# Softmax attention in a two-layer kernel: reciprocals taken over DRAM and applied by GpSimd, the causal mask added by VectorE

## The reference, cut to what matters

```python
latent_kv = x @ w_kv_down
kv = latent_kv @ w_kv_up
k, v = (kv[..., :HD], kv[..., HD:])
q = (x @ w_q).reshape(Bx, Tx, N_HEAD, HEAD_SIZE)
scale = HEAD_SIZE ** (-0.5)
att = jnp.einsum('bqhd,bkhd->bhqk', q, k) * scale
causal = jnp.tril(jnp.ones((Tx, Tx), dtype=bool))
att = jnp.where(causal, att, -jnp.inf)
att = jax.nn.softmax(att, axis=-1)
y = jnp.einsum('bhqk,bkhd->bqhd', att, v)
y = y.reshape(Bx, Tx, HD)
return y @ w_out
```

## Time and profile before

| | us |
|---|---|
| median of 3 runs (1919.01 to 1919.22) | 1919.13 |
| the profiled execution | 1919.19 |
| its span, first to last instruction | 1917.1 |
| TensorE busy | 1703.5 (89%) |
| VectorE busy | 1362.2 (71%) |
| ScalarE busy | 1000.8 (52%) |
| GpSimd busy | 619.1 (32%) |
| softmax attention, its first product to its last division | 1196.1 to 1740.5 |

### The profile page before, as it was taken

The page is one execution under the profiler, slowest core; times in us unless marked ns, Lnnn a source line. Parts: engine busy times, 40 slices in busy tenths (PEclk is TensorE's granted clock), DMA queues, the critical chain, the costliest instruction groups (busy, mean ns, idle before and its releaser), DMA issues. The chain is left out here.

```text
span 1917.1 us, 42317 instructions
## 1 busy us (share of the span) xinstructions
PE 1703.5 (89%) x15702; PEld 1445.2 (75%) x15702; DVE 1362.2 (71%) x3230; ACT 1000.8 (52%) x2618; POOL 619.1 (32%) x975
## 2 busy tenths in 40 slices
PE   4599999899999999999988598999999999998895
PEld 3477778787877778877876365688888888888794
DVE  4688777877788777877775475566666666664777
ACT  2355555555555555565543354556566656652353
POOL 6455345543555335543451122000000000001653
PEclk9799999999999999999988799999999999999898
DMA  6212331323222332323320200990000000003232
GB/s 216 59 51 65 75 86 49 68 59 85 65 56 65 75 87 46 74 67 75 83 50 23 90 1 5 183 14 2 2 2 2 1 2 1 2 2 107 65 93 76
DMA packets 150338, 106.78 MB, mean 56 GB/s; under 512 B 34132, under 2 KB 138648, under 8 KB 149240
## 3 DMA queue, kind: packets, MB, share of 16 engines
q1 hardware_dynamic: 147640, 98.95, 23.7%
q0 software_dynamic: 2496, 5.13, 0.8%
HBM read 86.06 MB, written 17.99 MB: 54 GB/s over the span
## 5 line engine op out<-in xcount | busy, mean ns | idle before, releaser
L593 POOL TENSOR_TENSOR kfull<-kt,pair_rows 128x512 f32<-128x512 f32 x128 | 143.6, 1122 | 517.2 <-ACT kt L381 513.5
L361 PE MATMUL ps<-xT,taps 128*128 128x128 f32 x2048 | 276.8, 278 | 0.1
L853 ACT COPY wt<-ps 32x128 f32<-32x128 f32 x512 | 131.7, 257 | 263.9 <-PE ps L748 256.9
L361 PEld LDWEIGHTS ps<-xT,taps 128*128 128x128 f32 x2048 | 258.7, 196 | 7.6 <-issue 7.2
L1687 DVE TENSOR_REDUCE b_nmax<-ps 128x1 f32<-128x128 f32 (+7 forms) x256 | 180.6, 752 | 72.9 <-PE ps L1524 72.9
L896 DVE TENSOR_TENSOR prod<-ps,mt 128x128 f32<-128x128 f32 x512 | 147.4, 288 | 78.6 <-PE ps L759 62.7
L748 PE MATMUL ps<-ident,w 128*128 128x128 f32 x512 | 162.9, 318 | 34.6 <-ACT wt L853 18.5
L1664 POOL COPY b_spread<-b_inv 128x256 f32<-128x256 f32 x64 | 25.8, 402 | 513.2 <-DVE b_inv L1690 513.2
L899 DVE TENSOR_REDUCE w<-prod 128x32 f32<-128x128 f32 x512 | 146.5, 286 | 17.5
L748 PEld LDWEIGHTS ps<-ident,w 128*128 128x128 f32 x512 | 88.1, 172 | 84.9 <-DVE w L899 73.6
L1616 ACT ACTIVATE b_prob_long<-ps,b_nmax 128x1024 f32<-128x1024 f32 (+3 forms) x128 | 121.4, 953 | 55.7 <-DVE b_nmax L1687 55.7
(11 more groups left out here) (308 smaller groups left out, 3843.2 us busy)
## 6 DMA issues: line engine op xcount, KB each, us to landing
decay<-ends_dram SPq DMA_DIRECT2D x256, 128.0 KB, 5.5
gn<-near_dram SPq DMA_DIRECT2D x32, 384.0 KB, 6.9
slots_dram<-zero SPq DMA_DIRECT2D x1, 9216.0 KB, 59.3
rr<-rates_dram SPq DMA_DIRECT2D x32, 256.0 KB, 4.5
sq<-rstd_dram SPq DMA_DIRECT2D x16, 512.0 KB, 3.6
wtap<-in_taps SPq DMA_DIRECT2D x4, 1024.0 KB, 11.2
f_w<-in_f_w SPq DMA_DIRECT2D x2, 2048.0 KB, 10.4
s_xb<-slots_dram SPq DMA_DIRECT2D x46, 64.5 KB, 1.8
```

The lines of the kernel that those rows point to most:

```text
L361: mm = pe.matmul(part, lhsT=taps[:, tap, t * P:(t + 1) * P], rhs=xT[:, :, columns(at_next) - LOOK + tap:columns(at_next) - LOOK + tap + TS ...
L593: nc.gpsimd.tensor_tensor(kfull[:, n % 4, :, :], kt[:, n % 2, :].unsqueeze(1).to_broadcast([P, G, P]), cst["pair_rows"][:, :].unsqueeze(2) ...
L853: nc.scalar.copy(wt[rows, b, :], ps[rows, 2, 0:P]).then_inc(wt_kept[b], 1)
```

## The change

Four things, in one diff:

1. The reciprocals no longer pass through GpSimd's copy, TensorE's transpose and ScalarE's copy. SyncE stores the 128x4 reciprocals to DRAM (`recips_dram`, two slots) and, when they have landed, loads them back with two broadcasts over 64 partitions each, into `recipT` in the layout of the values.
2. ScalarE copies the values out of bank 7 into `yT` (`keep_values`), and GpSimd multiplies `yT` by `recipT` in place. TensorE's values of the next unit wait for ScalarE's copy (`o_kept`). VectorE's `divide` is gone.
3. TensorE's mask products are gone. VectorE adds the mask to the diagonal tile in the bank and waits for that addition (`masked`) before it takes the row's maximum. The waits for copied banks now stand in `scores`, at the first product into each bank.
4. SyncE's two fill transfers are issued by ScalarE instead, after its first eight projection copies and ahead of its first exponential.

Besides, VectorE's reciprocal waits until the store of the unit two before has landed, and the 16-bit identity is no longer built in the first stage.

```diff
@@ softmax_attention
-        spread = sb("spread", [P, 2, 4, AD])
-        recipT = sb("recipT", [P, 2 * P])
+        recipT = sb("recipT", [P, 2, 2 * P])
+        recips_dram = nc.dram_tensor("recips_dram", (2, 4, P), F32).ap()
...
+        def y_of(w):
+            hp, b, k = units[w]
+            return y_row[:, hp, b, k:TT - k:TT - 1 - 2 * k, :, :]
@@ tensor
-                def masks(w):
-                    for long in (False, True):
-                        for h in range(2):
-                            n = tiles(w, long)
-                            if w:
-                                for c, (of_long, lo, hi, bank) in enumerate(chunks(w - 1)):
-                                    if bank == (2 * h + 1 if long else 4 + h):
-                                        wait_kept_chunk(w - 1, c)
-                            pe.matmul(scores_of(w, long, h)[:, (n - 1) * P:n * P], lhsT=cst["ident16"][:, :],
-                                      rhs=cst["above_diag"][:, :], start=True, stop=False, skip_group_check=True)
...
-                                if w and not diagonal and c0 == 0:
+                                if w and c0 % 512 == 0:
                                     for c, (of_long, lo, hi, bank) in enumerate(chunks(w - 1)):
-                                        if bank == 2 * h:
+                                        if bank == (2 * h + c0 // 512 if long else 4 + h):
                                             wait_kept_chunk(w - 1, c)
...
-                                               rhs=kT[rows, f, b * T + c0:b * T + c1], start=not diagonal, stop=True,
+                                               rhs=kT[rows, f, b * T + c0:b * T + c1], start=True, stop=True,
...
                     if w:
-                        pe.wait_ge(y_done, w)
+                        pe.wait_ge(o_kept, w)
...
-                def turn_recips(w):
-                    pe.wait_ge(spread_done, w + 1)
-                    for long in range(2):
-                        mm = pe.transpose(ps[:, 7, (2 + long) * P:(3 + long) * P],
-                                          spread[:, w % 2, 2 * long:2 * long + 2, :].rearrange("p h c -> p (h c)"),
-                                          cst["ident"][:, :])
                     mm.then_inc(o_done, 1)
@@ scalar
-                def keep_recips(w):
+                def keep_values(w):
                     act.wait_ge(o_done, w + 1)
-                    nc.scalar.copy(recipT[:, :], ps[:, 7, 2 * P:4 * P]).then_inc(recip_kept, 1)
+                    nc.scalar.copy(y_of(w), ps[:, 7, 0:2 * P].rearrange("p (i n t) -> p i n t", i=2,
+                                                                        n=P // TS)).then_inc(o_kept, 1)
...
+                slots = blank[2].rearrange("(k p) e -> p k e", p=P)
+                act.wait_ge(fill_made, 2)
+                nc.scalar.dma_start(slots[:, :, 0:C], blank[1][:, :].unsqueeze(1).to_broadcast(
+                    [P, slots.shape[1], C])).then_inc(filled, 16)
+                nc.scalar.dma_start(slots[:, :, C:ROW], blank[0][:, :].bitcast(F32).unsqueeze(2),
+                                    allow_slow_non_contiguous=True).then_inc(filled, 16)
                 for w in range(W):
                     for j in range(4):
                         exponent(w, j)
@@ sync
-                sp.dma_start(slots[:, :, 0:C], ...)  and  sp.dma_start(slots[:, :, C:ROW], ...)
+                for w in range(W):
+                    slot = recips_dram[w % 2]
+                    if w >= 2:
+                        sp.wait_ge(y_done, w - 1)
+                    sp.wait_ge(recip_done, w + 1)
+                    sp.dma_start(slot.rearrange("j q -> q j"), inv[:, w % 2, :],
+                                 allow_slow_non_contiguous=True).then_inc(recip_stored, 16)
+                    sp.wait_ge(recip_stored, 16 * (w + 1))
+                    for h in range(2):
+                        sp.dma_start(recipT[AD * h:AD * h + AD, w % 2, :].rearrange("c (l q) -> c l q", l=2),
+                                     slot[h:4:2, :].partition_broadcast(AD)).then_inc(recip_in[w % 2], 16)
@@ gpsimd
-                    pool.wait_ge(recip_done, w + 1)
-                    nc.gpsimd.tensor_copy(spread[:, w % 2, :, :], inv[:, w % 2, :].unsqueeze(2).to_broadcast(
-                        [P, 4, AD])).then_inc(spread_done, 1)
+                    pool.wait_ge(recip_in[w % 2], 32 * (w // 2 + 1))
+                    pool.wait_ge(o_kept, w + 1)
+                    nc.gpsimd.tensor_tensor(y_of(w), y_of(w), recipT[:, w % 2, :].rearrange(
+                        "p (i n t) -> p i n t", i=2, n=P // TS), ALU.mult).then_inc(y_done, 1)
@@ vector
                         dve.wait_ge(s_done, 4 * w + j + 1)
+                        n = tiles(w, j // 2)
+                        diagonal = scores_of(w, j // 2, j % 2)[:, (n - 1) * P:n * P]
+                        nc.vector.tensor_tensor(diagonal, diagonal, cst["above_diag"][:, :], ALU.add).then_inc(masked, 1)
+                        dve.wait_ge(masked, 4 * w + j + 1)
                         nc.vector.tensor_reduce(nmax[:, w % 2, j:j + 1], scores_of(w, j // 2, j % 2), axis=AX.X, op=ALU.max,
                                                 negate=True).then_inc(max_done, 1)
                     dve.wait_ge(exp_done, 4 * w + 4)
+                    if w >= 2:
+                        dve.wait_ge(recip_stored, 16 * (w - 1))
                     nc.vector.reciprocal(inv[:, w % 2, :], total[:, w % 2, :]).then_inc(recip_done, 1)
-                    if w:
-                        divide(w - 1)
```

More of the change, by code:

```diff
@@ L1555, in values @@
                                 cols = slice(AD * h, AD * h + AD)
-                                pe.matmul(ps[cols, 7, long * P:(long + 1) * P], lhsT=v[:, f, b * TT + j, cols],
-                                          rhs=probT[:, at_probT(w, long, h * n + j), :], start=(j == 0), stop=(j == n - 1),
-                                          skip_group_check=True)
-                def turn_recips(w):
-                    pe.wait_ge(spread_done, w + 1)
-                    for long in range(2):
-                        mm = pe.transpose(ps[:, 7, (2 + long) * P:(3 + long) * P],
-                                          spread[:, w % 2, 2 * long:2 * long + 2, :].rearrange("p h c -> p (h c)"),
-                                          cst["ident"][:, :])
+                                mm = pe.matmul(ps[cols, 7, long * P:(long + 1) * P], lhsT=v[:, f, b * TT + j, cols],
+                                          rhs=probT[:, at_probT(w, long, h * n + j), :], start=(j == 0),
+                                               stop=(j == n - 1), skip_group_check=True)
                     mm.then_inc(o_done, 1)
@@ L1585, in _ @@
                 pe.wait_ge(piece_kept_v, 4)
-                masks(0)
                 for w in range(W):
@@ L1597, in _ @@
                         next_piece(w, n)
-                    if w + 1 < W:
-                        masks(w + 1)
                 values(W - 1)
-                turn_recips(W - 1)
             @block.scalar
@@ L1633, in _ @@
                     if w:
-                        keep_recips(w - 1)
+                        keep_values(w - 1)
                     hp = w // PW
@@ L1644, in _ @@
                                 "p (j t) -> p j t", t=P)).then_inc(t_kept_a, 1)
-                keep_recips(W - 1)
+                keep_values(W - 1)
             @block.sync
             def _(sp):
-                slots = blank[2].rearrange("(k p) e -> p k e", p=P)
-                sp.wait_ge(fill_made, 2)
-                sp.dma_start(slots[:, :, 0:C], blank[1][:, :].unsqueeze(1).to_broadcast(
-                    [P, slots.shape[1], C])).then_inc(filled, 16)
-                sp.dma_start(slots[:, :, C:ROW], blank[0][:, :].bitcast(F32).unsqueeze(2),
-                             allow_slow_non_contiguous=True).then_inc(filled, 16)
+                for w in range(W):
[9 more added lines that the diff above has]
+                                     slot[h:4:2, :].partition_broadcast(AD)).then_inc(recip_in[w % 2], 16)
+                for slot in range(2):
+                    sp.wait_ge(recip_in[slot], 32 * (W // 2))
                 sp.wait_ge(filled, 32)
@@ L2224, in program @@
                "pair_rows": sb("pair_rows", [P, G]), "lower": sb("lower", [P, NE, NE]),
[L2225 to L2226 removed]
+               "above_diag": sb("above_diag", [P, P], BF16)}
         stream = sb("stream", [P, 1 + NT, C])
```

24 lines of the change are left out of this document (5 added, 19 removed).

## The result

The changed kernel takes 2207.56 us (median of 4 runs, 2202.77 to 2209.53), the kernel before 1919.18 beside it: a ratio of 1.1496 [1.1474, 1.1518], 288 us slower. The forecast was 1947 us with a range of 1928 to 1976. The sign was right, the size was not: the time lies far outside the range, and past the rival that was priced highest (2062).

What follows compares the result with a forecast made beforehand. The prediction took TensorE, the busiest engine, as the bound. Onto 1919.19 us it summed 45.6 (hold) + 2 (clock) - 22 (loop) + 2 (tail) = +27.6, giving 1947 us, range 1928 to 1976 for 8 in 10.

Steps and rivals of the forecast that it cites:

- The sign: Whole kernel: slower than before, with a chance of 0.86.
- the rival that was priced highest: Rival 3, on the reciprocals' trip over DRAM, priced at 2062 us; chance 0.04.
- the one on ScalarE, GpSimd and SyncE: Attention loop: these engines' new work is hidden; the reciprocals' DRAM trip takes 5 to 9 us and costs nothing.
- the hold: Attention start: issuing the second fill transfer holds ScalarE 50.80 us, delaying the first exponentials; +45.6 us.
- Rival 3: Loop: the DRAM trip is slower than a unit; at 10 us a unit +115 us, 2062 us; chance 0.04.
- the clock behind it: After some 45 us without work TensorE restarts at the lower clock; +2 us, bounds 0 and 4.
- the mask: Each VectorE mask addition with its wait, ahead of the row's maximum, takes 0.325 us.
- the loop: Attention units: work off TensorE less new waits gives -1.4 us per four units, times 16: -22 us.
- the tail: End of the attention stage: last reciprocal, DRAM trip and product end later; +2 us, bounds 0 and 5.
- Kind 0: First of four unit kinds in turn; TensorE saves 0.52 us but waits 0.74 for the fourth exponential.
- Rivals 1, 2 and 4: ScalarE not held, 1899 us (0.12); VectorE's additions set the pace, 1969 or 1985 (0.10); hold about half, 1919 (0.02).
- a late bank of 0.4: After kind 3, the fourth unit kind, ScalarE's copies end later; the next unit's long scores wait 0.4 us.

Runs made afterwards that it cites:

- rows16: Changed kernel with the reciprocals stored as 128 rows of 16 bytes instead of 512 scattered elements of 4 bytes; 1953.84 us, ratio 1.0186.
- same_engine: Changed kernel with the 512 single 4-byte elements laid so that the four of one partition are neighbours; 2163.04 us, ratio 1.1160.
- best_mix: best_dve with only the two long rows of Kind 0 units masked by TensorE inside the score products; 1933.65 us, ratio 0.9975.
- deep: Changed kernel with 64 source slots for reciprocals, so VectorE never waits for a store; 2207.58 us, ratio 1.1496.
- mask_dve: Kernel before with only the masks moved from TensorE's products to VectorE's additions; 1917.94 us, ratio 0.9994.
- best_pe: best_dve with the masks left on TensorE; 1914.69 us, ratio 0.9970.
- spaced: Changed kernel with the 512 elements of a store 64 bytes apart in DRAM; 1969.09 us, ratio 1.0257.
- best_dve: Changed kernel with 16-byte-row stores, one 256 KB load, two GpSimd products of 64 partitions, eight reciprocal slots, fill on SyncE again; 1911.92 us, ratio 0.9962.

## Why the prediction was wrong

**The step that failed** is the one on ScalarE, GpSimd and SyncE: "The store is bounded by the fill's second transfer, 18432 such elements: 512/18432 of 50.8 us of issue is 1.4 us, of 29.4 us 0.8, and 1.4 us for a small store", and from it "The trip costs nothing in the loop". The count of elements and their size were taken over from the fill, but not where they land. The fill's elements are the last of rows of 129 floats, 516 bytes apart; the store's stand 4 bytes apart. The runs show that such a store lands in 10.0 us, and one with its elements 64 bytes apart in 1.81 (3.8 to 4.4 right behind loads), against a price taken of 1.4 to 2.2. The scale was right for spaced elements that stand clear of loads, and 4.5 to 7 times too small for the packed ones of this kernel.

**What it cost.** The changed kernel less rows16 is 2207.56 - 1953.84 = 253.7 us. In the two profiled executions (249 apart) it stands as 218.8 from first to last scores, 25.6 in the tail (38.6 against 13.0), and some 5 in other places, 3.8 of it in the last stage, which took between 175.8 and 180.7 us in the profiled executions, whatever the kernel, leaving out the slower chip of same_engine and best_mix. With the hold, +50.8, and the rest of the change, -16.0, the sum is 288.5; measured were 288.4. As the -16.0 was itself what rows16 left over, the sum had to come out; what supports it is the -15.7 and +1.6 of the traces. The sign of the forecast was not luck, since the hold alone outweighs that gain, but most of the 288 us came by another way.

**Rival 3 came true**, with a chance of 0.04: store and issue over 7 us, VectorE's reciprocal waiting for stores, turned tiles uncopied. Its place and its condition were right. Its price was low (10 us a unit; measured 11.5, and it left out the tail). The reason held against it, 1.4 us for a small store, was a row of another pattern (`rstd_dram`, 4 KB in rows of 32 bytes), and 0.04 was too little for a cost that no row of before showed. Nor did the range reach to it.

**TensorE's lower clock** in the loop (0.87; a score product took 475 ns in the mean, before 366) goes with the rests: rows16, without them, has 1.00. deep shows that it doesn't set the time: there TensorE is far ahead of SyncE, and the time is the same.

**The terms that held:** the hold and the clock behind it, 45.6 + 2 forecast, +50.8 measured, of which the first unit has 48.5 (its exponentials start at 1263.60, forecast 1262.1, as the issue took 53.3 us instead of 50.8) and the last stage 2.1; the mask 0.33 us against 0.325; the loop -1.2 a round of four against -1.4, the tail +1.6 against +2 with a quick store. The loop's term as a whole was too large, -22 against -15.7, as a round gains less and the last eight units gain nothing. Kind 0 became longer than laid out (8.58 - 0.52 + 0.74 = 8.80, in rows16 9.02), and kinds 1 to 3 together came out as laid out (22.9 us). With the quick store of rows16 the time is 1953.84, inside the range of the forecast. Rivals 1, 2 and 4 are out: ScalarE was held, and a mask costs 0.33 us. By parts, a round of four gains 0.42 us by the masks (mask_dve) and 0.59 by the reciprocals' new way (best_pe), 1.0 of the 1.2 of both. That kind 0's chain grows by 0.4 us beyond two masks in mask_dve goes with scores of 2.60 us instead of 2.22, and 0.30 of it is the wait for VectorE's copy; the forecast had a late bank of 0.4 there, but let only TensorE wait for it and not the chain. In rows16 the scores are as long (2.65) without a wait of that size; why is open.

## What to carry to other kernels

Price a small transfer by its pattern at the far end, not by its count of elements: a store that transposes in DRAM puts single elements side by side, and here that took 10.0 us for 2 KB where rows of 16 bytes took 1.4. The Trainium skill, page "DMA: Bandwidth & Descriptors", section "Rules for kernel authors", says to rearrange so that the last dimension is contiguous; the runs agree (1.4 against 10.0), though the number of single elements by itself cost only 0.4 us (spaced against rows16). Let the reader of the table (here GpSimd's product) do the turning. A transfer chain with a wait between its links (store, landed, load, next store) is a loop with a period of its own: write that period beside the compute loop's before calling it hidden, and keep large transfers of small elements off the queue of any engine that has timely work behind them.

## What was not expected of the hardware

- Landing of 512 elements of 4 bytes in DRAM: 1.81, 1.90, 2.51 and 10.0 us when they lie 64, 32, 16 and 4 bytes apart; 8.85 at 4 bytes in another order. The packets of the packed store end 2.2 us behind its start, and its semaphore is complete 7.4 us later.
- A store of 2 KB issued on SyncE's queue right behind the fill held the queue itself for 31.54 us (best_dve), where it takes 0.32 later.
- The issue of the fill's second transfer held its engine for 50.8 to 55.1 us over the runs, on SyncE and on ScalarE alike.
- Two single mask products inside a stream of 64-row score products made the scores 0.9 us longer (3.46 against 2.58 us, to the start of the next products).
- GpSimd's product over 64 partitions took 0.86 us in the mean where that over 128 took 0.73. It also read its reciprocals at a step of 16 bytes; no run parts the two.
